# Finding the ones of an adjacency matrix in packed bytes, loaded by converting DMAs

## The reference

```python
mask = adj.astype(jnp.float32) + jnp.eye(n)
q = (h @ Wq.T + bq).reshape(n, 8, 32)          # k and v likewise
scores = jnp.einsum('nhd,mhd->hnm', q, k) / jnp.sqrt(32.)
scores = jnp.where(mask[None] == 0, -1e9, scores)
ctx = jnp.einsum('hnm,mhd->nhd', jax.nn.softmax(scores, axis=-1), v).reshape(n, 256)
h1 = layer_norm(h + ctx @ Wo.T + bo)
out = layer_norm(h1 + jax.nn.relu(h1 @ W1.T + b1) @ W2.T + b2)
```

## Time and profile before

| | us |
|---|---|
| median of 3 runs | 555.56 |
| lowest and highest run | 549.12, 556.79 |
| the profiled execution | 549.15 |
| its span between first and last instruction | 547.3 |
| mean granted clock of TensorE | 0.954 |

### The profile page before, as it was taken

The page is one execution under the profiler, slowest core; times in us unless marked ns, Lnnn a source line. Parts: engine busy times, 40 slices in busy tenths (PEclk is TensorE's granted clock), DMA queues, the critical chain, the costliest instruction groups (busy, mean ns, idle before and its releaser), DMA issues.

```text
span 547.3 us, 7383 instructions
## 1 busy us (share of the span) xinstructions
PE 474.0 (87%) x2306; PEld 376.7 (69%) x2306; DVE 430.6 (79%) x978; ACT 218.0 (40%) x540; POOL 266.9 (49%) x391
## 2 busy tenths in 40 slices
PE   5999997958599899989989998979886788789994
...
GB/s 276 416 420 416 345 213 319 402 412 423 353 342 331 252 368 323 335 326 346 307 325 376 270 302 146 200 94 238 185 115 274 178 230 150 53 156 21 20 0 43
DMA packets 40059, 140.94 MB, mean 257 GB/s; under 512 B 4936, under 2 KB 17096, under 8 KB 35920
## 3 DMA queue, kind: packets, MB, share of 16 engines
...
q10 hardware_dynamic: 1792, 1.85, 1.0%
...
## 4 chain that ended last, share of the span: by engine, by line
PE 42%; DVE 34%; DMA 8%; ACT 6%; issue 6%; POOL 2%; SPq 0%; POOLq 0%; ACTq 0%; DVEq 0%
DVE found L509 14%; PE ps L1094 11%; PE ps L1809 10%; PE ps L1107 9%; DMA xT_all<-in_xT 4%; PE ps L848 3%; PE ps L1074 3%; DVE stats L1168 2%; DVE slots L691 2%; DVE slots L704 2%; DMA adj_buf<-in_adj 2%; DVE slots L623 2%; DVE slots L713 1%; DMA early<-in_wqkvT 1%; ACT early L1158 1%
## 5 line engine op out<-in xcount | busy, mean ns | idle before, releaser
L509 DVE FIND_INDEX8 found<-ones,adj_buf 128x8 uint32<-128x4105 int32 (+5 forms) x40 | 138.7, 3467 | 0.0
L1094 PE MATMUL ps<-xT_all,w 128*128 128x512 f32 (+1 forms) x320 | 121.0, 524 | 2.8 <-ACT xT_all L1148 2.5
L1107 PE MATMUL ps<-w,xT_all 128*128 128x256 f32 x512 | 118.5, 385 | 3.1 <-ACT xT_all L1148 3.1
L1107 PEld LDWEIGHTS ps<-w,xT_all 128*128 128x128 f32 x512 | 96.0, 192 | 15.9 <-ACT xT_all L1148 3.8
L1094 PEld LDWEIGHTS ps<-xT_all,w 128*128 128x128 f32 x320 | 59.1, 195 | 44.8 <-issue 35.6
L1019 POOL DMA_INDIRECT slots<-kv_table,col_of x54 | 55.9, 1036 | 45.7 <-DVE col_of L592 34.4
L1148 ACT ACTIVATE xT_all<-ps,col_table 128x512 f32<-128x512 f32 (+1 forms) x80 | 47.8, 603 | 57.4 <-PE ps L1094 57.4
L1809 PE MATMUL ps<-early,xT_all 128*128 128x256 f32 x256 | 59.4, 393 | 6.2 <-DMA early<-in_wqkvT 6.1
L1809 PEld LDWEIGHTS ps<-early,xT_all 128*128 128x128 f32 x256 | 49.9, 197 | 14.2 <-DMA xT_all<-in_xT 5.3
L962 ACT ACTIVATE xT_all<-ps,col_table 128x256 f32<-128x256 f32 (+1 forms) x38 | 14.5, 432 | 85.6 <-PE ps L851 85.5
L1011 POOL DMA_INDIRECT slots<-kv_table,found x32 | 34.9, 1089 | 26.7 <-PE ps L851 9.1
(11 more groups left out here) (180 smaller groups left out, 821.0 us busy)
## 6 DMA issues: line engine op xcount, KB each, us to landing
...
kv_table<-slots POOLq DMA_DIRECT2D x7, 1024.0 KB, 11.6
xT_all<-in_xT SPq DMA_DIRECT2D x13, 512.0 KB, 13.5
slots<-kv_table SPq DMA_DIRECT2D x12, 512.0 KB, 9.8
...
out_dram<-early SPq DMA_DIRECT2D x6, 512.0 KB, 5.0
...
```

The source lines that it names most:

```text
L509: last = nc.vector.max_index(dst, ones8[:], part)
L1094: last = nc.tensor.matmul(ps[:, q["bank"] + f % 2, 0:q["g"] * P], w1[:, k, f * P:(f + 1) * P], q["h1T"][:, k, :], start=(k == 0), stop=(k ...
L1107: nc.tensor.matmul(to, q["ffT"][:, f, j * P:(j + 1) * P], w2[:, f, :], start=(f == 0), stop=False)
```

## The change

A tile's adjacency goes into SBUF as one byte for each column instead of four: the same 2 MB are read from HBM, and the DMA converts int32 to uint8 on the way. Such a DMA is issued from POOL, so `load_adj` moves from SP's queue to POOL's. There are four buffers of 4096 bytes a row where there were two of 16 KB; the wait becomes `wait(pool, hunted, s + 1 - BUFFERS)`. The first four loads stand in POOL's opening (two among its constants, two behind the first two stores of the key and value table), the next two behind the gathers of step 0, and in step i the loads for step i + 3 behind the query gathers for step i + 1. Tile 0 keeps its int32 load from SP and its search.

The bytes of a row are read as 1024 float32 words of four columns each. `nc.vector.max` (MAX8) gives the eight largest words of a unit, `max_index` their positions. `columns_dve` then forms, for each of the 8 words and its 4 bytes, position x 4 + byte number + 1 + start of the unit, multiplies by the byte (0 or 1), and one more MAX8 over the 32 products gives the columns, largest first, with 0 for a missing one. Aligned gathers now wait for `listed` instead of `hunted` or `aligned_ready`. The hit test is `> 0` instead of a comparison with the unit's limit; the start addition (528), the copy (531) and the third mask step (558) go away for all but tile 0.

```diff
+PACK = 4
+BUFFERS = 4
...
-        adj_buf = [sb(f"adj_buf{i}", [P, 1 + N + FOUND], I32) for i in range(2)]
+        adj_bytes = sb("adj_bytes", [P, 2 * BUFFERS, N], U8)
+        adj_words = flat(adj_bytes[:]).bitcast(F32).rearrange("p (b w) -> p b w", w=N // PACK)
+        spare = flat(adj_bytes[:, BUFFERS:, :]).bitcast(F32)
+        at_word, at_column, at_first = [UMAX * FOUND * n for n in (1, 2, 2 + PACK)]
+        top_words = spare[:, 0:at_word].rearrange("p (u f) -> p u f", f=FOUND)
+        word_at = spare[:, at_word:at_column].bitcast(U32).rearrange("p (u f) -> p u f", f=FOUND)
+        column = spare[:, at_column:at_first].rearrange("p (w b) -> p w b", b=PACK)
+        first_column = spare[:, at_first:at_first + 7 * FOUND * PACK].rearrange("p (w b) -> p w b", b=PACK)
         found0 = sb("found0", [P, TILE0.U, max(ROOM)], U32)
         found = sb("found", [P, OTHERS, FOUND], U32)
-        aligned_idx = sb("aligned_idx", [P, OTHERS], U32)
...
-        adj_loaded = [sem("adj_loaded0"), sem("adj_loaded1")]
+        adj_loaded = [sem(f"adj_loaded{i}") for i in range(BUFFERS)]
...
+        def find_dve(dve, q, ti):
+
+            s = q.h + ti
+            words = adj_words[:, s % BUFFERS, :]
+            dve.wait_ge(adj_loaded[s % BUFFERS], (s // BUFFERS + 1) * 16)
+            units_of = range(q.nu) if q.nu > 1 else (ti,)
+            for u in units_of:
+                lo, hi = (q.edges[u] // PACK, q.edges[u + 1] // PACK) if q.nu > 1 else (0, N // PACK)
+                nc.vector.max(top_words[:, u, :], words[:, lo:hi]).then_inc(hunt, 1)
+            for u in units_of:
+                lo, hi = (q.edges[u] // PACK, q.edges[u + 1] // PACK) if q.nu > 1 else (0, N // PACK)
+                dve.wait_ge(hunt, hunts_before(q) + u + 1)
+                last = nc.vector.max_index(word_at[:, u, :], top_words[:, u, :], words[:, lo:hi])
+            last.then_inc(hunted, 1)
+
+        def columns_dve(dve, q):
+
+            n = hunts_before(q) + q.U
+            words = q.U * FOUND
+            c = column[:, 0:words, :]
+            at = COLUMNS_AT[q.nu] * FOUND
+            dve.wait_ge(hunted, q.h + q.T)
+            index = word_at[:, 0:q.U, :].rearrange("p u f -> p (u f)").unsqueeze(2).to_broadcast([P, words, PACK])
+            nc.vector.scalar_tensor_tensor(c, index, float(PACK), first_column[:, at:at + words, :], ALU.mult, ALU.add).then_inc(hunt, 1)
+            dve.wait_ge(hunt, n + 1)
+            ones = top_words[:, 0:q.U, :].rearrange("p u f -> p (u f)").bitcast(U8).rearrange("p (w b) -> p w b", b=PACK)
+            nc.vector.tensor_tensor(c, c, ones, ALU.mult).then_inc(hunt, 1)
+            dve.wait_ge(hunt, n + 2)
+            for u in range(q.U):
+                last = nc.vector.max(hits(q)[:, u, :], flat(column[:, u * FOUND:(u + 1) * FOUND, :]))
+            last.then_inc(listed, 1)
...
-            nc.vector.tensor_tensor(m, raw, units(limit, q).unsqueeze(2).to_broadcast([P, q.U, q.room]), ALU.is_le).then_inc(mask_link, 1)
+            raw = hit if q.first else hits(q)
+            dve.wait_ge(listed, q.p + 1)
+            if q.first:
+                nc.vector.tensor_tensor(m, raw, units(limit, q).unsqueeze(2).to_broadcast([P, q.U, q.room]), ALU.is_le).then_inc(mask_link, 1)
+            else:
+                nc.vector.tensor_scalar(m, raw, 0.0, None, ALU.is_gt).then_inc(mask_link, 1)
...
-            if q.nu == 1:
-                pool.wait_ge(hunted, q.h + q.T)
-            else:
-                pool.wait_ge(aligned_ready, total_prepared(lambda p: 1 if p.nu > 1 and p.A else 0, q.p + 1))
+            pool.wait_ge(listed, q.p + 1)
...
-        def load_adj(sp, s):
-            wait(sp, hunted, s - 1)
+        def load_adj(pool, s):
+            wait(pool, hunted, s + 1 - BUFFERS)
             t = SEARCHED[s]
-            sp.dma_start(adj_buf[s % 2][:, 1:1 + N], adj[t * P:(t + 1) * P, :]).then_inc(adj_loaded[s % 2], 16)
+            pool.dma_start(adj_bytes[:, s % BUFFERS, :], adj[t * P:(t + 1) * P, :]).then_inc(adj_loaded[s % BUFFERS], 16)
...
-            load_adj(sp, 0)
             load_xT(1)
             load_xT(2)
-            load_adj(sp, 1)
             load_xT(3)
             sp.dma_start(adj0[:, 1:1 + N], adj[0:P, :]).then_inc(adj0_loaded, 16)
             for c in range(4, GROUPS):
                 load_xT(c)
-            load_adj(sp, 2)
-            load_adj(sp, 3)
             for dst, src in ((wo, woT.rearrange("(k p) n -> p k n", p=P)), (w1, w1T.rearrange("(k p) n -> p k n", p=P)),
                              (w2, w2T.rearrange("(k p) n -> p k n", p=P))):
                 sp.dma_start(dst[:], src).then_inc(s_weights, 16)
             for name, src in (("g2", g2), ("be2", be2)):
                 sp.dma_start(rows[name][:], src.to_broadcast([P, D])).then_inc(s_weights, 16)
             load_own(sp, STEPS[0])
-
-            sp.wait_ge(got_edges[STEPS[0].par], 2 * STEPS[0].U * 16)
-            load_adj(sp, 4)
-            load_adj(sp, 5)
...
-                if i + 3 < NB:
-                    for ti in range(STEPS[i + 3].T):
-                        load_adj(sp, STEPS[i + 3].h + ti)
...
+            load_adj(pool, 0)
+            for at, edges in ((0, (0, 0)), (2, EDGES[3][:2]), (4, EDGES[1][:3])):
+                for u, edge in enumerate(edges):
+                    part = first_column[:, (at + u) * FOUND:(at + u + 1) * FOUND, :]
+                    nc.gpsimd.iota(part, [[0, FOUND], [1, PACK]], base=1 + edge, channel_multiplier=0, **exact)
...
             last.then_inc(s_const, 1)
+            load_adj(pool, 1)
...
                 pool.dma_start(kv_tiles[:, g * GROUP:(g + 1) * GROUP, :], kv_stage[c % STAGES]).then_inc(s_kv_out[c % STAGES], 16)
+                if c < 2:
+                    load_adj(pool, 2 + c)
...
             gather_queries(pool, STEPS[0])
+            for ti in range(STEPS[2].T):
+                load_adj(pool, STEPS[2].h + ti)
...
                     gather_queries(pool, soon)
+                if i + 3 < NB:
+                    for ti in range(STEPS[i + 3].T):
+                        load_adj(pool, STEPS[i + 3].h + ti)
```

139 lines of the change are left out of this document (57 added, 82 removed).

## The result

The changed kernel is slower: 556.73 us median of 20 runs (553.83 to 559.31) against 549.99 us (547.38 to 557.70) of the kernel before in 20 runs beside them, a ratio of 1.011 with a 95% interval of 1.008 to 1.014. The forecast was 539.5 us with a range of 522 to 575: the time lies in the range, on the wrong side of the start.

The account below looks back on a forecast made before the run. The bound was taken to change by stretch: PE, then DMA, then DVE first in the wide steps, then engines waiting in turns. Gains 3 + 7 + 6 = 16 us off the 555.56 us median gave 539.5 us, range 522 to 575.

Parts of the forecast that it names:

- the search's total: Search of a tile on DVE: costs 2.5 us after the change and saves 1.9 to 2.0 us.
- near 390: DVE's busy time over the whole kernel after the change, in us, from 430.6 before.
- factor f: DMA engines' cost of a converting load relative to a plain one: taken as 1, kept between 0.9 and 2.
- rivals 1 and 4: 1: converting load slow, DMA becomes the bound, slower, chance 0.20. 4: converting loads cheaper, about 526 us, chance 0.08.
- rival 2: POOL stalls when issuing loads, cancelling most of the 16 us gain: about 552 us, chance 0.12.
- the second stretch: Steps 0 to 2, 85.8 to 152 us: 3 us gained from a DVE wait and the earlier residual.
- the third stretch: Seven wide steps, 152 to 317 us: 7 us gained as PE stops waiting for late DVE; ends 0 and 10.3.
- Ends: 0.7 and 1.5 us: Limits on the added DVE time per batch for forming columns, taken as 0.95 us.
- The fourth stretch: 317 to 492 us: seven searches, 9.8 us, four on the chain that ended last; 6 us gained.
- the last: Last stretch, 492 us to the end, with no search left: 0 us gained.
- Rival 3: PE or the DMA queue takes over at once: no change, about 549 us, chance 0.10.
- its own range is 528 to 545: Range in us given to the 539.5 us forecast itself, apart from the rivals.

Follow-up runs that it names:

- e1: Changed kernel with the loads for step 2 issued after the remaining query stores, and those in steps 0 and 1 after that step's stores: 550.18 us, ratio 1.000.
- e6: Changed kernel with loads where they were, but the query-table stores issued by ACT in its own queue instead of POOL: 546.08 us, ratio 0.989.
- e3: Kernel before with the search of every undivided tile cut from 4105 to 2696 elements, loads and queues untouched: 551.03 us, ratio 1.000.
- e4: Kernel before with the search of every undivided tile cut from 4105 to 520 elements: 556.81 us, ratio 1.004.
- e2: Changed kernel with query stores ahead of loads, each load reading only 512 KB instead of 2048 KB and converting nothing: 540.66 us.
- e7: Kernel before with half of the second feed-forward product left out, so less TensorE work: 545.19 us, ratio 0.988.

## Why the prediction was wrong

**What held.** MAX8 (1.22), the search's total, DVE's busy time (387.2 for "near 390"). DVE no longer waits for adjacency once step 0 has begun. The factor f of the converting load is near the 1 that was taken: over the whole execution the load's queue changes from the first pair of lines (before) to the second (after; packets, MB, share of the span):

```profile
q1 hardware_dynamic: 24896, 95.03, 46.2%
q0 software_dynamic: 13328, 43.55, 23.1%
```

```profile
q0 software_dynamic: 17792, 59.80, 54.3%
q1 hardware_dynamic: 20432, 30.02, 15.4%
```

q1 falls from 252.9 to 85.7 us and q0 rises from 126.4 to 302.0, with 31 loads in each: 5.4 us of all engines for a plain load and 5.7 for a converting one, if the rest of q0 costs what it did before. By the page of e1 it is 5.5. So f is 1.02 to 1.05, and rivals 1 and 4 are both wrong. POOL issues a load in 0.61 us, 31 of them, so rival 2 is wrong as well.

**The step that failed first: the second stretch, "+3, ends -5 and +9".** It gave -7.6, outside its own ends. The prediction did weigh gathers that stand behind 4 MB in their own queue, and found 12.5 us between the loads and the next gather. It did not ask the same of the query stores. They were the first thing behind the loads in POOL's program (83.78 and 84.92), and the cost, 10.7 us a pair of loads, stood in the text. The prediction names nothing that waits behind a store; but its buffer is one of four that ACT must refill, and ACT, DVE and PE follow in order. That ACT already waited up to 4.6 us for these stores in the kernel before was in the waits of that stretch and is not in the prediction. e1 and e6 take this loss away from two sides.

**Then the third stretch, "3.5 x 1.94 = 7 us" (it gave -2.5).** Even with the first steps mended it is +1.7 (e1) and +0.2 (e6), and e3 with the same relief and nothing else has +2.9. Two terms of this step were wrong. One: the statistics' 1.6 us delay was put down to the search, while the chain ahead of them on DVE is the step's softmax; and it was the longest of three (0.4, 1.6 and 0.7 us in the kernel before), taken for every pair. The delay stayed (in the trace of after attention ends at 236.1 and the statistics at 237.8 are again 1.7 us late), and PE's wait at L1100 is 6.1 us in three as before. Two: the wide step has no single bound. Relieving DVE (e3, e4), the DMA engines (e2), or TensorE (e7) left the seven steps between 160.9 and 166.5 us. DVE's 157.8 of 165 us was read as "first"; it was one of several engines in a ring, and PE was 2% behind it. ACT's part of the ring was relieved in no run.

**And a cost was set at nothing whose cover the change itself removed**: POOL's products under the search. "Ends: 0.7 and 1.5 us" for the columns became 1.7 us in the mean of the wide steps (L543 1.1 instead of 0.25), and 2.8 in three of the seven.

**The fourth stretch, "6, ends 2 and 10", and the last, "0".** They gave +3.6 and -2.1. The cut between them is an instruction of DVE, which may stand elsewhere against PE's work once DVE has less to do, so they are better read together, from step 10 to the end: 231.5 us before, 230.0 after, 233.1 in e1, 231.2 in e6, 230.2 in e3. e3, whose divided searches are as long as before, gives 1.3 us here by itself. The kernels with the seven shorter searches give between -1.6 and +1.5 us, below the lower end of 2 and not told apart from nothing. "Four of them are on the chain that ended last" was true and no measure of what their shortening gives; that the chain is one way through a ring whose other ways are nearly as long is argued from the wide steps, as no run relieved the single ones by DVE alone.

In sum: 3 + 7 + 6 = 16 was forecast; by the same stretches -7.6 - 2.5 + 3.6 - 2.1 and -0.2 ahead of step 0 make -8.8 against the span's -8.9. Rival 3 (PE or the DMA queue takes over: third 3, second -2, fourth 5) came nearest in kind. Its second stretch was too mild by 5.6 us and its third by 5.5. It was given 0.10, and a time within 2% of the start, which is what came, 0.22.

Two things of the numbers themselves. The forecast was taken off 555.56 us, a median of three runs; the kernel before has 549.99 in twenty, so 539.5 was 1.9% under it and not 2.9%. And "its own range is 528 to 545" is narrower than the ends of the sum's own terms: with -5, 0 and 2 the same sum gives 3 us more than the start, 558.6, and with 9, 10.3 and 10 it gives 526.3.
